# Conv block on one core: four score banks and two ring banks in all slots, values in the projections' bank

## The reference

```python
def _L0_conv_ref(x, Wq, bq, Wk, bk, Wv, bv):
    t = x.reshape(B, C, S).transpose(0, 2, 1)
    q = t @ Wq.T + bq
    k = t @ Wk.T + bk
    v = t @ Wv.T + bv
    q = q.reshape(B * NUM_HEADS, S, hd)
    k = k.reshape(B * NUM_HEADS, S, hd)
    v = v.reshape(B * NUM_HEADS, S, hd)
    scores = jnp.einsum('gqd,gkd->gqk', q, k) / jnp.sqrt(jnp.asarray(hd, x.dtype))
    attn = jax.nn.softmax(scores, axis=-1)
    wv = jnp.einsum('gqk,gkd->gqd', attn, v)
    wv = wv.reshape(B, S, NUM_HEADS, hd).transpose(0, 2, 3, 1)
    return wv.reshape(B, C, W, H)
...
x = x + _L0_conv_ref(_gn(x), L0_conv_Wq, L0_conv_bq, L0_conv_Wk, L0_conv_bk, L0_conv_Wv, L0_conv_bv)
x = x + _L1_conv_ref(_gn(x), L1_conv_weight, L1_conv_bias, L1_conv_mask_weight, L1_conv_filter, 1)
```

## Time and profile before

| | us |
|---|---|
| median of three runs | 2551.43 (2547.43 to 2552.2) |
| the profiled execution | 2547.02 |
| its span, first to last instruction | 2545.2 |
| TensorE matmul busy | 2440.3 (96%) |
| VectorE busy | 1947.8 (77%) |
| ScalarE busy | 1146.8 (45%) |
| GpSimd busy | 1156.7 (45%) |

### The profile page before, as it was taken

The page is one execution under the profiler, slowest core; times in us unless marked ns, Lnnn a source line. Parts: engine busy times, 40 slices in busy tenths (PEclk is TensorE's granted clock), DMA queues, the critical chain, the costliest instruction groups (busy, mean ns, idle before and its releaser), DMA issues.

```text
span 2545.2 us, 38904 instructions
## 1 busy us (share of the span) xinstructions
PE 2440.3 (96%) x13768; PEld 916.8 (36%) x13768; DVE 1947.8 (77%) x2617; ACT 1146.8 (45%) x2059; POOL 1156.7 (45%) x998
## 2 busy tenths in 40 slices
PE   6899999999999999999999999988999999999999
PEld 2233333333333333333333333322444444444444
DVE  5887887888888788788878898976856967967415
ACT  4455556555555556555555554565232132132100
POOL 1376577567567657756755764653121030030000
PEclk9999999999999999999999999999999999999999
DMA  4213232131322313213132231322534634633534
GB/s 128 73 53 87 68 99 81 37 106 53 95 76 74 87 47 111 82 45 106 50 98 76 75 110 36 106 71 72 191 135 174 236 132 165 231 133 133 205 110 165
DMA packets 162783, 267.95 MB, mean 105 GB/s; under 512 B 80160, under 2 KB 80288, under 8 KB 162592
## 3 DMA queue, kind: packets, MB, share of 16 engines
q1 hardware_dynamic: 162320, 264.41, 31.5%
q10 hardware_dynamic: 272, 1.05, 0.1%
HBM read 195.54 MB, written 52.69 MB: 98 GB/s over the span
## 4 chain that ended last, share of the span: by engine, by line
PE 76%; DVE 16%; issue 4%; ACT 1%; DMA 1%; POOL 1%; SPq 0%; DVEq 0%; ACTq 0%; POOLq 0%
PE bank L854 29%; PE bank L761 13%; PE bank L684 12%; PE bank L735 12%; DVE nmax L1297 6%; PE bank L694 5%; DVE prob_sum L1290 4%; PE bank L705 4%; DVE val L1309 1%; PE bank L715 1%; DVE xn_lo L1274 1%; DMA q_top<-shift 1%; ACT prob L936 1%; PE bank L748 1%; DVE xn L1367 1%
## 5 line engine op out<-in xcount | busy, mean ns | idle before, releaser
L1297 DVE TENSOR_REDUCE nmax<-bank 128x1 f32<-128x512 f32 x1024 | 650.9, 680 | 201.6 <-PE bank L705 188.5
L936 ACT ACTIVATE prob<-bank 128x512 f32<-128x512 f32 x1024 | 555.2, 594 | 467.1 <-PE bank L735 465.5
L854 PE MATMUL bank<-v,u_slab 128*128 128x512 f16 x3456 | 746.9, 379 | 0.0
L1119 POOL TENSOR_TENSOR prob_sum<-prob_sum,prob 128x512 f32<-128x512 f32 x354 | 489.8, 1384 | 256.7 <-ACT prob L936 254.6
L761 PE MATMUL bank<-prob,val 128*64 128x512 f32 x2048 | 495.9, 605 | 0.0
L854 PEld LDWEIGHTS bank<-v,u_slab 128*128 128x128 f16 x3456 | 338.1, 98 | 406.9 <-issue 0.8
L1290 DVE TENSOR_TENSOR prob_sum<-prob_sum,prob 128x512 f32<-128x512 f32 x326 | 364.2, 1117 | 23.1 <-POOL prob_sum L1125 21.5
L705 PE MATMUL bank<-k_hi,q_hi 64*128 64x512 f16 x1024 | 200.2, 385 | 35.5 <-DVE nmax L1297 34.7
L735 PE MATMUL bank<-q_hi,k_hi 64*128 64x512 f16 x1024 | 196.4, 378 | 26.4 <-ACT prob L936 26.3
L761 PEld LDWEIGHTS bank<-prob,val 128*64 128x64 f32 x2048 | 124.2, 136 | 237.8 <-issue 186.5
L735 PE MATMUL bank<-q_lo,k_hi 64*128 64x512 f16 x1024 | 196.2, 378 | 8.6 <-DMA q_top<-shift 8.5
(11 more groups left out here) (146 smaller groups left out, 2876.5 us busy)
## 6 DMA issues: line engine op xcount, KB each, us to landing
u_slab<-u_scratch SPq DMA_DIRECT2D x72, 1024.0 KB, 4.7
xs<-x SPq DMA_DIRECT2D x28, 1024.0 KB, 5.5
tile<-x_scratch SPq DMA_DIRECT2D x26, 1024.0 KB, 6.5
u_scratch<-u_w SPq DMA_DIRECT2D x96, 192.0 KB, 2.9
den_sb<-recip_scratch SPq DMA_DIRECT2D x128, 128.0 KB, 2.9
x_scratch<-xr SPq DMA_DIRECT2D x16, 1024.0 KB, 4.3
xr<-x SPq DMA_DIRECT2D x15, 1024.0 KB, 7.8
res<-x_scratch SPq DMA_DIRECT2D x14, 1024.0 KB, 7.3
```

Source lines behind the costliest of these rows:

```text
L854: mm = pe.matmul(bank_at(pos, co)[:].rearrange("p (i n) -> p i n", i=2), slab[:, l, c, co * P:(co + 1) * P], image[v][:, 2 * c:2 * c + 2, ...
L936: act.activation(prob[:, (2 * u + e) % 8], score_bank[score_turn[16 * h + 2 * u + e]][:], ACT.Exp, scale=float(D) ** -0.5).then_inc(s1["ex ...
L1119: nc.gpsimd.tensor_tensor(acc, in0, prob[:, (2 * kc + 1) % 8], ALU.add).then_inc(s1["sum1"], 1)
L1297: dve.tensor_reduce(nmax[:, seg, part:part + 1], src[:], AX.X, ALU.max, negate=True)\
```

## The change

The scores have four banks in every slot: 0, 1, 2 and 5. The ring has two, 3 and 4, and serves the maximum pairs, the row sums and the statistics; a small class `Ring` takes the bank that was taken longest ago, and TensorE and VectorE each hold one. The values leave the ring: they are projected into qk_bank, with a semaphore `value_ready` of their own, after the last query evacuation and after the value before has been copied out. VectorE's value item no longer waits for its own end, since the increment `value_out` on the copy is what TensorE waits for.

```diff
-def bank_turn(n, period, banks=3):
-    left = (0, 4, 2)[period % banks]
-    def bank_of(k):
-        k %= period
-        return k % banks if k < period - left else (k - period) % 2
-    return bank_of(n), next(d for d in range(1, period) if bank_of(n - d) == bank_of(n))
+class Ring:
+    def __init__(self, banks):
+        self.n, self.banks, self.seen = 0, banks, [-3, -2, -1]
+    def turn(self):
+        b = min(range(self.banks), key=lambda k: self.seen[k])
+        ago, self.seen[b] = self.n - self.seen[b], self.n
+        self.n += 1
+        return self.n - 1, b, ago
...
-        short = h % HPH == HPH - 1 and h < B * HPI - DIRECT
-        b = min(range(4 if short else 3), key=lambda k: seen[k])
+        b = min(range(4), key=lambda k: seen[k])
...
-        score_bank = sc_bank + [qk_bank]
+        score_bank = sc_bank + [v_ring[2]]
...
-            ring = Count()
+            ring = Ring(2)
             def take():
-                b, ago = bank_turn(ring.n, PER_RING)
-                if ring.n >= ago:
-                    pe.wait_ge(s1["ring_free"], ring.n + 3 - ago)
-                dst = v_ring[b]
-                ring.n += 1
-                return dst
+                n, b, ago = ring.turn()
+                if n >= ago:
+                    pe.wait_ge(s1["ring_free"], n + 3 - ago)
+                return v_ring[b]
...
                     if which == 0 and j == 0:
-                        pe.wait_ge(s1["exp_done"], 4 + 16 * HPH * (t - 1))
+                        pe.wait_ge(s1["value_out"], 4 * t)
...
             def project_value(t, half, g):
                 pe.wait_ge(s1["xn_split"], 2 + 4 * (t + 1))
-                dst = take()
+                pe.wait_ge(s1["qk_out"], 1 + 8 * (t + 1))
+                pe.wait_ge(s1["value_out"], 4 * t + g)
+                dst = qk_bank
...
-                mm.then_inc(s1["ring_full"], 1)
+                mm.then_inc(s1["value_ready"], 1)
...
-                        if score_turn[n] == 3:
-                            pe.wait_ge(s1["qk_out"], 1 + 8 * (h // HPH + 2))
...
                 if kc == 0:
                     pe.wait_ge(s1["qk_out"], 1 + 16 * B)
+                    pe.wait_ge(s1["value_out"], B * HPI)
...
             def value_item(h, half, g):
-                src = item()
-                dve.scalar_tensor_tensor(out=val[half][:, g], in0=src[:], scalar=1.0 / WSCALE, in1=bv_row[:],
+                dve.wait_ge(s1["value_ready"], h + 1)
+                dve.scalar_tensor_tensor(out=val[half][:, g], in0=qk_bank[:], scalar=1.0 / WSCALE, in1=bv_row[:],
                                          op0=ALU.mult, op1=ALU.add).then_inc(s1["value_out"], 1)
-                dve.wait_ge(s1["value_out"], h + 1)
-                dve.sem_inc(s1["ring_free"], 1)
```

More of the change, by code:

```diff
@@ L216, in build @@
             "u_in", "u_act", "u_pool",
-            "u_out0", "u_out1", "u_out2", "den_full", "pv_out", "den_out", "den_in", "recip_done", "recip_out", "recip_in", "o_done", "resid_done", "x1_stored", "value_out")}
+            "u_out0", "u_out1", "u_out2", "den_full", "pv_out", "den_out", "den_in", "recip_done", "recip_out", "recip_in", "o_done", "resid_done", "x1_stored", "value_ready", "value_out")}
         def statistics(dve, signal, step, cols):
@@ L323, in build @@
         stage = prob[:].rearrange("p (a k) n -> p a k n", a=2)
-        PER_RING = HPI * (16 + 1) + 2 * HPH + 2
         def tokens(s):
@@ L1254, in _ @@
         def _(dve):
-            ring = Count()
+            ring = Ring(2)
             step = Count()
             def item():
-                dve.wait_ge(s1["ring_full"], ring.n + 1)
-                src = v_ring[bank_turn(ring.n, PER_RING)[0]]
-                ring.n += 1
-                return src
+                n, b, _ = ring.turn()
+                dve.wait_ge(s1["ring_full"], n + 1)
+                return v_ring[b]
             step2 = Count()
```

## The result

The changed kernel takes **2631.95 us** (median of 4 runs, 2629.34 to 2633.65) against 2550.61 us (2547.43 to 2552.2) for the kernel before beside it: ratio 1.0319, 95% interval 1.0307 to 1.0331, **81.3 us slower**. The forecast was 2640 us in a range of 2602 to 2667. Its profiled execution spans 2630.0 us, 84.8 more than that of before.

A forecast was written before the change was run, and what follows sets the result against it. TensorE, working in written order, was taken to bound the kernel. Six images +71, image 6 and half of 7 +17, start +8.4, end -6.5 gave +90 on 2547.0 us, 2637; forecast 2640 us, range 2602 to 2667.

The forecast's parts named there:

- The rule: With two ring banks, a maximum pair right behind another waits for both its reductions: 1.86 us start to start, not 1.25.
- slots 4 and 5: The pair after unit 4's scores moves by 0.60 us and the row sums wait 0.07 more: 0.67 each.
- Slot 1: Row sums' copy, crowded pair and statistics add 1.83 us; up to 0.72 returns where slot 2 waited for the shift row.
- Slots 2 and 6: Slots with values: row sums, their copy and the pair after unit 4's scores cost 1.42 us each.
- Slots 3 and 7: Slots without a projection, where TensorE runs into the reductions: pairs and row sums cost 2.65 us each.
- The fourth score bank in the six images: Gain 0: at unit 0 of slots 0 and 4 the scores then wait for the shift row's DMA, not the exponential.
- The start: Before the first slot, four values queue through one bank and the first pairs wait for second reductions: +8.4 us.
- Images 6 and 7 and the end: Ring waits partly swallowed: 11 us for image 6, 6 for image 7's first half; last four slots -6.5.
- The signs: Reduction waits near 100 us, over 200 times; (4,c) pair 0.60 later; row landing unchanged; first pair near 60.5; image near 226.
- Rival 1: The new TensorE waits are mostly swallowed: only +35 to +60 us, 2582 to 2611; chance 0.13.
- Rival 3: Faster, -15 to -25 us: VectorE, relieved at the values, ends second reductions in time and exponential waits go; chance 0.04.
- Rival 2: More than the sum, +120 to +150 us: short gaps in slots 3 and 7 halve TensorE's clock; chance 0.10.

The follow-up runs named there:

- B: A with a ring of two banks in place of three, three score banks, the eighth bank idle: 2641.57 us, ratio 1.0354.
- H: Changed kernel with the maximum pair behind unit 4's scores moved into unit 3's projection, in slots with a projection: 2608.29 us, ratio 1.023.
- C: Kernel before, shift row sent to a scratch tensor and nothing waiting for it (maximum not subtracted): 2538.15 us, ratio 0.9948.
- D: Changed kernel, shift row sent to a scratch tensor and nothing waiting for it (maximum not subtracted): 2618.66 us, ratio 1.0265.
- A: Kernel before (ring of three, three score banks, fourth in short slots alone) with only the values moved to the projections' bank: 2540.82 us, ratio 0.9962.
- E: D with three score banks in place of four (fourth in short slots alone), ring of two, no shift row: 2637.7 us, ratio 1.0343.
- F1: Changed kernel with the first four values alternating between the queries' bank and the weighing's: 2630.55 us, ratio 1.0317.
- F2: F1 run once more, beside the changed kernel on the same chip: 2627.68 us against 2631.57.
- G: Changed kernel with the row sums moved out of the ring into the bank of the queries and keys: 2602.9 us, ratio 1.0214.
- I: Changed kernel with the edits of F1, G and H together: 2577.01 us, ratio 1.0106.
- L: Changed kernel run again, unchanged, against the kernel before: 2631.57 us, ratio 1.032.

## Why the prediction was right

**The rule held.** "A pair right behind a pair costs 1.86 us in place of 1.25" is the 1.86 of 1106.53 to 1108.39, and the slots 4 and 5 grew by 0.60 in each of the six images. B shows that the ring of two makes the loss, and H that the pairs' part of it goes where they are spaced by more than 1.86. The 0.07 that I added for the row sums in slots 4 and 5 was not there: the part of the slot ahead of (4,c) did not move by 0.01.

**Values and slots, term by term.** Slot 0: 1.02, as forecast. Slot 1: 1.83 forecast; inside it the shift is 1.66, since the statistics at (4,d) add 0.65 and not 0.82. In slot 1 of image 4, TensorE, they wait 0.76 us:

```profile
1025.01 0.39 PE L702 MATMUL bank<-k_hi,q_hi 64*128 64x512 f16 x2 [0.61 <-DVE nmax L1292]
1026.17 0.39 PE L284 MATMUL bank<-mv,cst 128*128 128x8 f32 x2 [0.76 <-DVE nmax L1292]
```

C and D show the same 1.66 without the row (medians 29.31 and 30.97); with it, up to 0.8 is taken back where the row held slot 2 before, as forecast, so that the median is 1.46. Slots 2 and 6: 1.42 forecast, 1.32 and 1.06 measured. The pair at (3,a) moved by 1.18 and the pair at (4,c) by 1.33 (forecast: 1.21 and 1.42), but slot 6 had a further wait before at (6,a), which A also shows, and 0.28 of the loss vanished in it. Slots 3 and 7: 2.65 forecast, and in slot 3 of image 4 +0.37, 0.96, 1.61, 2.21 and 2.81 at its pairs from (2,a) on; the first step is the 0.09 that I had mis-sized. Six images: 66.8 for 71.

**The fourth score bank in the six images** gives nothing, as argued from the row that lands 0.05 us ahead of part 1. D against E shows the hidden gain: 9.4 us between the first slot and the end of image 5 without the row.

**The start** came to 9.70 for 8.4. The first pair starts 4.44 later (55.73 to 60.17; I had it near 60.5). Of the rest some 1.7 is the clock: the pre-slot stretch has a second spell at half clock in the changed kernel, from 76.9 on, that the kernel before had not. The windows view there (columns as under D) has the granted clock at 0.51:

```profile
76.90:80.30 3.40, 3.40 (x10) 1.19 (x9) 1.29 (x2) 0.00 (x0) 0.00 (x0) 0.51 0.01 2
```

**Images 6 and 7 and the end** are the mis-sized terms. The step was "part of the ring waits is swallowed: 11 for image 6, 6 for the first half of image 7"; it was 8.4 and 3.7, so more was swallowed. (For a half image of slots 0 to 3 the rule gives 6.9, not the 6.6 that I wrote.) In the last four slots I forecast -6.5 and it was -3.8. The exponential waits of the earlier trace rows are gone as said, but new waits stand there. In the changed kernel, 1757 to 1877.6 us (the last four slots begin at 1778.9; 2.5 of the 9.7 lie ahead of that):

```profile
PE bank L702 <- DVE nmax L1292: 9.7, 16, 0.7
PE bank L730 <- DMA q_top<-shift: 2.3, 3, 1.0
PE bank L744 <- ACT prob L932: 1.8, 2, 0.9
PE bank L850 <- DMA u_slab<-u_scratch: 0.8, 1, 0.8
```

The 2.3 us for the row were not in my sum: in the last image, too, it takes over where the exponential let go. Slot by slot, each up to the next one's part 1 and the last up to the convolution, the four changed by -2.3, +2.3, -0.3 and -3.5 us, where my terms put -2.8, +0.8, +0.8 and -5.5 (these add to -6.7; I had written -6.5). The last slot's missing 2.0 are two waits that my sum did not have: 0.85 us at 1859.66, where the row sums from the exponentials (line 744) wait for one of them, and 0.78 at 1877.46, where the convolution's first matmul waits for its transforms (line 850), each some 0.17 more from start to start. That the convolution has its first transforms ready was true at the old pace and no longer at the new. That the bank is worth its most at the end is shown by B against the changed kernel: they stand 3.4 us apart the other way at the end of image 5 and 9.1 this way at the convolution.

**The signs.** The first pair (60.17 for 60.5), the pair at (4,c) and the row's landing came as said. An image of the medians takes 224.3 us, not 226. The waits for a maximum reduction are 118 us with those of the single items, near the 100 forecast, but 168 in number and not over 200.

**The sum** of the errors: +1.3 at the start, -4.2 in six images, -4.9 behind them, +2.7 at the end, 84.8 for 90. So the total is nearer than its parts: 4.9 of 17 us behind the six images and 2.7 of 6.5 at the end were wrong, with opposite signs, and that they cancel in part is luck. The medians stand 81.3 apart and not 84.8, since the profiled execution of before took 3.6 us less than the median and that of after (2631.76) only 0.2 less.

**The rivals.** Rival 1 (mostly swallowed) had its place only in the second halves of the last images. Rival 3 (faster, by VectorE running ahead) was half a mechanism: the values' move does relieve the ring and VectorE and gives 9.6 us with three banks; with two the pair at (4,c) still waits for both reductions. What the move is worth in a ring of two was not run. My sum held that relief inside the slots (the 0.22 at the values) and never priced the move for itself, which is why A surprised me. Rival 2 (clock) did not come: the stretch of the slots runs at full clock, but for one place, below. Nor did VectorE's additions fall worse: its 326 additions of line 1285 (1290 before) took 338.9 us in place of 364.2.

## What to carry over

A ring of banks between two engines must be counted in items in flight where the producer sends two right behind each other: at two banks for pairs each engine waits out the other's start latency (here 0.6 us for a pair right behind a pair), and a single item whose evacuation is queued behind long work holds the pair behind it. Together the two made 101 us here. Before giving a bank to one consumer, look at what releases it next: here the gain in the first six images stood behind a DMA that landed 0.05 us before the work, and only removing that row as well made it visible. A good extra tenant for a bank is one whose uses are far apart (the values in the projections' bank). And a place for an item in the middle of a long accumulation in another bank can do what a third ring bank does: with it the slots 4 and 5 came back to 28.53 and 28.52 us, from 29.10, with two ring banks (28.51 and 28.49 before).

## What the runs showed of the hardware

**Half clock behind a long wait, but not always.** In the changed kernel the shift row came latest at the beginning of image 4: TensorE stood 2.19 us, then ran at half clock for 3.4 us, and that slot is 1.65 us longer than its fellows.

```profile
977.79 0.39 PE L730 MATMUL bank<-q_lo,k_hi 64*128 64x512 f16 x2 [2.19 <-DMA q_top<-shift]
978.02 0.59 PE L730 MATMUL bank<-q_top,spare 64*128 64x512 f16 x2
978.54 1.12 PE L757 MATMUL bank<-prob,val 128*64 128x512 f32 x2
```

```profile
977.70:982.00 4.30, 4.21 (x14) 0.99 (x16) 1.13 (x1) 1.10 (x3) 4.30 (x4) 0.60 0.00 0
```

The second run of the same kernel has the same late row (2.06 us) and the same spell. In F1 and F2 the row was late there too, by waits of 1.78 and 1.97 us, and the clock stayed full; B and G have neither. But a wait of 2.45 us at 1575.96 was followed by no spell in the first profile, and one of 2.53 us at the same place by one in the second. In images 1 to 5 of all fourteen traces no wait below 2 us was followed by a spell, the 0.6 us waits of the slots 3 and 7 among them. Elsewhere the length of the wait does not settle it: in E one of 1.96 us at 1600.41 was followed by a spell, in G one of 2.44 at 1546.97 and in I one of 3.19 at 1524.55 were not, and in the last two images some spells begin behind waits of 0.6 to 0.9 us in a row. A spell of 3.4 us cost some 1.7. The clock can also fall in the middle of a wait: in the kernel before, it is full from 73.7 to 74.7 and half from 74.8 on, while TensorE stands until 77.90 for the first shift row. The Trainium skill, TensorE: Matmul & The Clock Gate, section A second HAM failure mode: psum-queue depth-cycling, tells of a bf16 kernel in which short idles between groups that cycle through PSUM banks make the clock oscillate. That rule, which the prediction weighed, does not show in images 1 to 5, where waits of 0.6 us stand 1.86 apart in every slot 3 and 7 at full clock; in the last two images, where such waits are followed by spells, it may be at work, and no run separates the two.

**Why the row was late there.** SyncE's queue holds the row behind the load of the row sums' reciprocals, which waits for its own store. At that place and at slot 4 of the same image:

```profile
970.36 0.32 SPq L432 DMA_DIRECT2D recip_scratch<-recip_col  x1
973.50 1.12 SPq L435 DMA_DIRECT2D den_sb<-recip_scratch  x2
974.67 1.34 SPq L422 DMA_DIRECT2D q_top<-shift  x2
```

```profile
1086.98 0.34 SPq L432 DMA_DIRECT2D recip_scratch<-recip_col  x1
1088.39 1.13 SPq L435 DMA_DIRECT2D den_sb<-recip_scratch  x2
1090.35 1.33 SPq L422 DMA_DIRECT2D q_top<-shift  x2
```

From the store to the load it took 3.14 us in place of 1.41, the row left 1.17 us behind the load, and it took 3.12 us in place of 2.39 from its issue to the matmul that waits for it. The same reading at the beginning of the slots 0 and 4 in images 1 to 6 and of slot 0 in image 7 of this trace:

| slots | TensorE's wait for the row | store to load | load to row |
|---|---|---|---|
| eight | 0.51 to 0.55 | 1.40 to 1.42 | 1.95 to 1.98 |
| five | 0.84, 1.17, 1.25, 1.47, 2.19 | 2.48 to 3.14 | 1.17 |

So every late row of these left the queue right behind a load that had been held by its store. The slots ahead of the four longest waits are the ones that stand out, 23.11, 23.46, 22.78 and 24.05 us, where the others of the slots 3 and 7 take 21.9 to 22.3. The repeat L, F1 and G divide in the same way (store to load 2.47 to 2.97 where the wait is over 0.6 us, 1.39 to 1.43 elsewhere). Why the store takes longer at some places stays open, and no run tried to free the row from this queue; without the row the excess mostly disappears (slot 7 of images 1 to 5 takes 21.0 to 21.6 us in D and 21.9 to 24.1 in the changed kernel).
